# Three layers of an audio tower on one core: 258-token tiles with stacked scores against 512-token tiles with row-tiled scores

## The reference

```python
# 1. token mixer: per channel, over the time of a sequence
zf, zi, zh = x @ Wf + bf, x @ Wi + bi, x @ Wh + bh
diff = softplus(-zf) - softplus(-zi)
log_f, log_i = -softplus(diff), -softplus(-diff)
log_val = concat([log(0.5), log_i + log_g(zh)])        # now 257 positions
a_star = concat([0, log_f])
h = exp(a_star + cumlogsumexp(log_val - a_star))
# 2. attention with 8 heads of 16 channels; each sequence looks at the keys and
#    values of the one half a batch away
q, k, v = project(layernorm(h))
h = h + softmax(q @ swapped(k).T / sqrt(128)) @ swapped(v)
# 3. shared expert and 16 routed ones of 96 features, top 2 of 16
#    with f(a, b) = clip(a) * sigmoid(alpha * clip(a)) * scale * (clip(b) + shift)
x3 = layernorm(h)
z = f(x3 @ shared_w1 + shared_b1) @ shared_w2 + shared_b2
cw = normalised weights of the top 2 of softmax(x3 @ gate_w + gate_b), else 0
y = sum_e cw[e] * (f(x3 @ expert_w1[e] + expert_b1[e]) @ expert_w2[e] + expert_b2[e])
h = h + y + z
```

## Time and profile before

| | |
|---|---|
| median of three runs | 391.59 us |
| profiled execution: span from the first to the last instruction (the profile gives it no other time) | 388.2 us |
| instructions | 6049 |
| busy: TensorE, weight loads, VectorE, ScalarE, GpSimd | 316.8, 258.7, 298.8, 243.1, 158.3 us |
| granted TensorE clock, mean | 0.918 of 2.4 GHz |
| moved by DMA | 17.30 MB |

### The profile page before, as it was taken

One profiled execution on the slowest core, in us unless ns is written; L12 is line 12 of the kernel. 1 busy time (PEld: TensorE's weight loads), 2 busy tenths in 40 slices (PEclk: granted clock), 3 DMA queues, 4 the chain that ended last, 5 costly groups with the idle time before them and its releaser, 6 DMA issues. The chain is left out here.

```text
span 388.2 us, 6049 instructions
## 1 busy us (share of the span) xinstructions
PE 316.8 (82%) x2160; PEld 258.7 (67%) x2160; DVE 298.8 (77%) x500; ACT 243.1 (63%) x412; POOL 158.3 (41%) x125
## 2 busy tenths in 40 slices
PE   3427028986968999999899999979999998879873
PEld 1105027854667878788588787968787887768752
DVE  7894646722579969978998999887976788887990
ACT  2684521542684858597598685675773877485751
POOL 1000372101032874744348577342234445357752
PEclk9767755798986999999999999989999999999998
DMA  7500850000390000008400000075000000000000
GB/s 270 221 0 0 220 80 2 0 3 0 117 183 0 2 3 1 0 3 218 56 28 2 2 3 0 2 207 67 28 2 0 3 2 0 0 31 3 0 1 27
DMA packets 12414, 17.30 MB, mean 45 GB/s; under 512 B 984, under 2 KB 9184, under 8 KB 12256
## 3 DMA queue, kind: packets, MB, share of 16 engines
q1 hardware_dynamic: 12384, 16.91, 17.6%
HBM read 11.63 MB, written 5.28 MB: 44 GB/s over the span
## 5 line engine op out<-in xcount | busy, mean ns | idle before, releaser
L506 POOL TENSOR_TENSOR te<-tbuf,ubuf 128x516 f32<-128x516 f32 x52 | 73.8, 1424 | 50.4 <-DVE tbuf L882 27.6
L956 PE MATMUL slot<-xh,w1h 128*128 128x258 f32 x208 | 64.7, 311 | 13.0 <-DVE xl L865 4.0
L495 POOL TENSOR_TENSOR ubuf<-ubuf,cwb 128x516 f32<-128x516 f32 x24 | 34.3, 1429 | 67.2 <-ACT cwb L659 48.9
L956 PE MATMUL slot<-xh,w1l 128*128 128x258 f32 x208 | 59.9, 288 | 0.0
L956 PE MATMUL slot<-xl,w1h 128*128 128x258 f32 x208 | 59.8, 288 | 0.0
L956 PE MATMUL slot<-te,w 128*128 128x258 f32 x208 | 50.7, 393 | 4.2 <-POOL te L506 3.5
L956 PEld LDWEIGHTS slot<-xh,w1h 128*128 128x128 f32 x208 | 40.3, 194 | 19.4 <-issue 14.0
L882 DVE SCALAR_TENSOR_TENSOR tbuf<-tbuf,gbuf 128x516 f32<-128x516 f32 x52 | 48.3, 935 | 6.0 <-ACT tbuf L666 5.6
L781 DVE TENSOR_REDUCE mx<-slot 128x2 f32<-128x514 f32 x64 | 41.6, 687 | 12.6 <-PE slot L956 12.4
L956 PEld LDWEIGHTS slot<-te,w 128*128 128x128 f32 x208 | 39.6, 195 | 12.8 <-POOL te L506 6.4
L646 ACT ACTIVATE gbuf<-slot,cst 128x516 f32<-128x516 f32 x52 | 35.8, 690 | 19.2 <-PE slot L956 16.8
(11 more groups left out here) (161 smaller groups left out, 614.6 us busy)
## 6 DMA issues: line engine op xcount, KB each, us to landing
qs<-spill SPq DMA_DIRECT2D x12, 258.0 KB, 4.5
ks<-spill SPq DMA_DIRECT2D x24, 129.0 KB, 5.9
spill<-qhl SPq DMA_DIRECT2D x4, 516.0 KB, 2.8
spill<-khl SPq DMA_DIRECT2D x4, 516.0 KB, 3.4
pt<-in_w SPq DMA_DIRECT2D x1, 1664.0 KB, 9.5
xt<-in_x SPq DMA_DIRECT2D x4, 256.0 KB, 5.4
out<-osb SPq DMA_DIRECT2D x8, 128.0 KB
te<-in_sel SPq DMA_DIRECT2D x1, 832.0 KB, 11.0
```

The source lines that it names most:

```text
L495: g.tensor_tensor(ubuf[:, c % NB, :, :], ubuf[:, c % NB, :, :], cwb[:, :, :], ALU.mult).then_inc(S["ucw"], 1)
L506: g.tensor_tensor(te[:, c % NTE, :, :], tbuf[:, c % NB, :, :], ubuf[:, c % NB, :, :], ALU.mult)\
L956: return nc.tensor.matmul(out_, lhsT, rhs, start=start, stop=stop, **k)
```

## The change

The kernel is written anew around the same mathematics.

- **Tiles.** A unit has 2 x 256 = 512 tokens and no position 0. Since h is 0.5 there in every channel, its layer norm is 0, and so are its q, k and v: as a key it gives the score 0 (the products `e0` add its term to the denominator), as a query the plain mean of v. Its FFN is computed at the end for all eight sequences at once, in tiles of 8 columns (all pieces whose name begins with z, except `z` itself).
- **Mixer.** In logarithms: absolute value, exponential, logarithm on ScalarE, one product for half the difference of zi and zf (`lsum`, with `wd`), two scans, no reciprocal; all sums on VectorE for unit 0 and on GpSimd for the others, by `PART_BY` (`dw` always on VectorE).
- **Scores.** Nothing goes to memory and back. q and k are copied twice with every other head of 16 channels set to 0; a product takes 32 rows of them at partition 32t in f32, four of these (t = 0 to 3) one behind the other into four banks. The maximum goes into two rows of q through a transpose (`mz`, `nmt`, `nm`). The denominator's reciprocal is a logarithm and an exponential on ScalarE (`den`).
- **Experts.** 12 chunks hold 8 features of each of the 16 experts, so that partition p always belongs to expert p mod 16 and one tile `cwb` of routing weights serves all 12; a 13th chunk is the shared expert, with the weights in rows 96 to 111 for expert_b2. There are no selection products. The first bias is row 0 of the weights: `w1b` holds row 0 on all partitions, which is subtracted (`w1p`), and row 0 of the normalised input is set to 1. One half is now three products of 512 columns into one bank. The eviction clips at once (VectorE: all g, four of seven pairs of u; for the other pairs ScalarE copies and GpSimd clips). tanh, `gg`, the weighting `vc` (GpSimd) and `te` (now VectorE) run over pairs of chunks, 1024 elements.
- **PSUM and order.** Eight banks, each given by a table (`BANK_OF`), and a new `AT`.

The core of the difference:

```diff
-W = N + 1
+W = 2 * T
...
+GATE_BY = ("V", "V", "V", "V", "V", "V", "V")
+UP_BY = ("AG", "AG", "V", "AG", "V", "V", "V")
+CW_BY = ("G", "G", "G", "G", "G", "G", "")
+TE_BY = ("V", "V", "V", "V", "V", "V", "V")
+PART_BY = {"t": "VGGG", "d": "VGGG", "hg": "VGGG", "dw": "VVVV", "lf": "VGGG", "h1": "VGGG", "xl": "VVVV", "h2": "GGGG"}
+NY, NV, NT = 3, 3, 4
...
 AT = {
     "P": (
-        0, 2, 4, 3, 5, 6, 7, 8, 9, 13, 17, 11, 14, 15, 12, 16, 19, 23, 31, 32, 30, 25, 29, 26, 34, 35, 36, 37, 38, 39,
...
+        2, 1, 0, 3, 8, 11, 20, 15, 19, 21, 22, 26, 28, 29, 32, 30, 34, 23, 27, 31, 33, 39, 40, 35, 42, 45, 48, 52,
...
-            def stack_q(st, u):
-                if u == 0:
-                    sp.wait_ge(s_zero, 1)
-                ge(sp, "h2n", 2 * u)
-                sp.wait_ge(S["spill_q"], 16 * (u + 1))
-                for r, src in enumerate((0, 1, 0)):
-                    sp.dma_start(qs[32 * r:32 * r + 32, :, :, :].bitcast(F32),
-                                 spill[u][src].rearrange("(t p) s n -> p s t n", p=32)).then_inc(S["stack"], 16)
...
# TensorE
-            def max_(st, u, s, c, t):
-                name = ("max", s, c, t)
-                if (s, c, t) == (0, 0, 0):
-                    ge(pe, "stack", 16 * NSTACK * (u + 1))
-                    if u == 0:
-                        pe.wait_ge(s_zero, ZEROED)
-                        pe.wait_ge(s_hot, 1)
-                take(pe, st, name)
-                for i in range(2):
-                    last = mm(slot(st, name)[:, i, 0:W], qs[0:KR, s, t, c * P:(c + 1) * P], ks[0:KR, 1 - s, t, i, :])
-                fill(last, st, name)
...
+            def mx(u, s, c):
+                ps.released(pe, "q", u)
+                ps.released(pe, "k", u)
+                for t in range(PAIRS):
+                    ps.take(pe, "mx", u, s, c, t)
+                for i in range(2):
+                    for t in range(PAIRS):
+                        rows = slice(32 * t, 32 * t + 32)
+                        last = mm(ps.bank("mx", u, s, c, t)[:, i * T:(i + 1) * T], qt[rows, i, s, c * P:(c + 1) * P], kt[rows, i, 1 - s, :])
+                        if i:
+                            ps.fill(last, "mx", u, s, c, t)
...
-            def half_(st, u, c, k):
-                name = ("gu"[k], c)
-                ge(pe, "xl", u + 1)
-                if u == 0:
-                    pe.wait_ge(s_setd, SETUP)
-                take(pe, st, name)
-                for s in range(2):
-                    o = slot(st, name)[:, s, 0:W]
-                    mm(o, w1h[:, k, c, :], xh[:, s, :], stop=False)
-                    mm(o, w1h[:, k, c, :], xl[:, s, :], start=False, stop=False)
-                    last = mm(o, w1l[:, k, c, :], xh[:, s, :], start=False)
-                fill(last, st, name)
...
+            def half_(u, c, name, kind):
+                ge(pe, "xl", u + 1)
+                pe.wait_ge(s_w1l, W1_PARTS)
+                ps.take(pe, name, u, c)
+                o = ps.bank(name, u, c)[:, :]
+                cols = slice((2 * c + kind) * P, (2 * c + kind + 1) * P)
+                mm(o, w1h[:, cols], xh[:, u % 2, :], stop=False)
+                mm(o, w1h[:, cols], xl[:, u % 2, :], start=False, stop=False)
+                ps.fill(mm(o, w1l[:, cols], xh[:, u % 2, :], start=False), name, u, c)
...
-            def gate_half(st, u, c):
-                filled(act, st, ("g", c))
-                if c >= NB:
-                    ge(act, "gg", NF * u + c + 1 - NB)
-                release(a(gbuf[:, c % NB, :, :], slot(st, ("g", c))[:, :, 0:W], ACT.Identity, bias=par[:, B1G, c:c + 1]),
-                        st, ("g", c))
...
+            def up_copy(u, c):
+                n = NP * u + c // 2
+                ps.filled(act, "u", u, c)
+                te_done(act, n - NV)
+                last = a(vr[:, n % NV, c % 2, :], ps.bank("u", u, c)[:, :], ACT.Copy)
+                ps.release(last, "u", u, c)
...
+            def den(u, s):
+                tables(SET_EXP_LN)
+                ge(act, "pv", 4 * u + 2 * s + 2)
+                ge(act, "h2", 2 * (u - 1) + s + 1)
+                a(rden[:, s, :], ps.bank("o0", u, s)[:, T:W], ACT.Ln).then_inc(S["lden"], 1)
+                ge(act, "lden", 2 * u + s + 1)
+                a(rden[:, s, :], rden[:, s, :], ACT.Exp, scale=-1.0).then_inc(S["rd"], 1)
...
-            def clip_gate(st, u, c):
-                released(dve, st, ("g", c))
-                p = c % NB
-                v.tensor_scalar(gbuf[:, p, :, :], gbuf[:, p, :, :], fpar[:, GHI, c:c + 1], fpar[:, GLO, c:c + 1],
-                                ALU.min, ALU.max).then_inc(S["gclip"], 1)
...
+            def gate_evict(u, c):
+                n = NP * u + c // 2
+                ps.filled(dve, "g", u, c)
+                dve.wait_ge(s_par, PARS)
+                ge(dve, "gg", n - NY + 1)
+                r = col(c)
+                last = v.tensor_scalar(yr[:, n % NY, c % 2, :], ps.bank("g", u, c)[:, :], fpar[:, GHI, r:r + 1],
+                                       fpar[:, GLO, r:r + 1], ALU.min, ALU.max)
+                ps.release(last, "g", u, c)
...
+            def gg(u, k):
+                n = NP * u + k
+                ge(dve, "th", n + 1)
+                t = halves(k, tr, n % NT)
+                v.scalar_tensor_tensor(t, t, 1.0, halves(k, yr, n % NY), ALU.add, ALU.mult).then_inc(S["gg"], 1)
...
+            def w1p(u, k):
+                pool.wait_ge(s_w1s, 1)
+                pool.wait_ge(s_w1b, 16)
+                g.tensor_tensor(w1_raw[:, w1_part(k)], w1_raw[:, w1_part(k)], w1_row[:, w1_part(k)], ALU.subtract).then_inc(s_w1p, 1)
...
+            def up_clip(u, k):
+                n = NP * u + k
+                ps.released(pool, "u", u, chunks(k)[-1])
+                v_ = halves(k, vr, n % NV)
+                r = col(2 * k)
+                g.tensor_scalar(v_, v_, fpar[:, UHI, r:r + 1], fpar[:, ULO, r:r + 1], ALU.min, ALU.max).then_inc(S["ucg"], 1)
...
+            def weigh(u, k):
+                n = NP * u + k
+                clipped(pool, "u", UP_BY, n, "ucv", "ucg")
+                ps.released(pool, "cwb", u)
+                g.tensor_tensor(vr[:, n % NV, :, :], vr[:, n % NV, :, :],
+                                cwb[:, u % 2, :].unsqueeze(1).to_broadcast([P, 2, W]), ALU.mult).then_inc(S["vcg"], 1)
...
```

1755 lines of the change are left out of this document (973 added, 782 removed), and 112 rows, old and new, of tables (AT, BANK_OF, BY, ENGINES).

## The result

The changed kernel takes 325.18 us (median of four runs, 324.81 to 325.96) against 392.06 for the kernel before on the same chip (391.55 to 395.01): 0.8283 of its time, 95% interval 0.8251 to 0.8315. The forecast was 324 us. The profiled execution took 325.96 us with a span of 324.1, so 1.9 us lie around the span; the prediction's 3.4 compared a span with the median of other runs.

A forecast was written before the change was run, and what follows sets the result against it. It took ScalarE's list to set the opening, 90 us, and VectorE with 197 us at a share of 0.853 the rest, 231 us; with 3.4 us around the span that made 324 us, range 284 to 364.

The forecast's parts named there:

- The opening: Stretch ahead of the first 512-column half product: forecast to end at 90 us, against 108.66 before.
- with 7 us of waits: Opening: 8.4 us before ScalarE begins, 75 of its work and 7 of waits put the halves at 90 us.
- is hidden: Opening: loading and splitting the first-layer weights is covered by ScalarE's list; without that cover up to 12 us.
- TensorE's sum: Behind 90 us: halves, down, scores, position 0, tile shape changes and other products add up to 208 us.
- nothing here shows that four wide loads overlap: Scores: reason for taking 0.9 us per group of four, between bounds of 0.43 and 1.72; 34 us in all.
- VectorE's sum: Behind 90 us: VectorE's operations add up to 175 us, or 197 with `gg` and `te` stretched; 197 taken.
- The stretch of `gg` and `te`: VectorE behind 90 us: these operations slow as 935 to 695 while GpSimd works, 79 us instead of 59.
- 197/0.853 = 231 us: Behind 90 us: VectorE's 197 us at its earlier steady share of 0.853 gives 231 us.
- Rival 1: Everything packs: 0.43 us per score group, `gg` and `te` unstretched, halves from 80 us; 282 us, chance 0.20.
- Rival 2: Score row groups run one by one, 1.72 us per group, halves from 97 us; 357 us, chance 0.15.
- rival 4: Slower: row-tiled products do not pipeline, 0.76 us a product, halves at 123 us; 437 us, chance 0.05.
- Rival 3: Searched order does not fit real durations, VectorE's share falls to 0.72; 367 us, chance 0.12.

The follow-up runs named there:

- e3: Changed kernel with every score product (mx and st) issued twice into the same bank; 351.13 us against 325.18.
- e7: Changed kernel with GpSimd's eight `w1p` subtractions touching 8 instead of 416 columns each; 322.90 us against 325.18.
- e9: Changed kernel with all mixer sums of units 1 to 3 on VectorE instead of GpSimd; 337.02 us against 325.18.
- e8: Changed kernel with q and the first score pieces of unit 0 moved earlier in the order, in other banks; 323.00 us against 325.18.
- e10: e8's order carried on: all mx, both `nmt`, the first st and their softmax of unit 0 ahead of unit 3's token products; 332.33 us.
- e1: Changed kernel with VectorE's `te` multiplying only the first of the two chunks of a pair; 326.07 us against 325.18.
- e2: Changed kernel with each half made of two products instead of three (`w1l` product left out); 313.69 us against 325.18.
- e12: Changed kernel with e8's order and position 0's gate and up operands exchanged (8 columns stationary), in banks already free; 318.94 us against 325.18.
- e4: Changed kernel with score products issued two in a row on the same 32 rows instead of cycling over row groups; 325.98 us against 325.18.
- e6: Changed kernel with position 0's 78 narrow products spread, four behind each 512-column half product, instead of one block; 334.28 us against 325.18.

## Why the prediction was right, and where it was not

It was right in direction, in size and in where the gain would come from (behind the first half product). Its two parts were off by 20 and 17 us in opposite directions, so that 324 is partly luck.

**The opening, 90 us forecast, 109.7 measured.** ScalarE's list was sized well: 75 forecast, 69.8 busy. What failed is the step "with 7 us of waits". ScalarE is 0.64 busy ahead of the first half product, not above 0.8, and is idle for 40 us in all, 31 of them beyond the 8.4 ahead of its first work that the prediction allowed. It is a chain that crosses every engine: e3 (more TensorE work), e7 (less GpSimd work), e9 (more VectorE work), e8 and e10 (the order alone) all moved its end, by -3 to +11 us. A sum of the fullest engine's list is only a lower bound where four engines feed each other through eight banks. In 40 to 75 us TensorE's granted clock is 0.67, too, and 16 score records take 2.09 us in place of 1.15.

**The weights preparation "is hidden": half right.** No engine that computes waits for a transfer after 6.8 us. But leaving most of `w1p` out brought 3.1 us (e7), and `w1l` on VectorE took 12.9 us, not 8 x 0.6, in the engine that is fullest in the opening.

**TensorE's sum, 208 forecast, about 209 measured,** from row to row of its timeline. Inside it: scores 20.9 instead of 34 (a group 0.53, not 0.9); halves, with what changes of shape and low clock add to them, about 81 instead of 68 (0.233 apart, which was the upper bound, and a first one of 0.34 behind a change); position 0 18.5 instead of 12.5, since the clock falls in it; down 47 instead of 45; value and ones 21.9 instead of 20.9; the products of 512 f32 columns 8.4 and the small shapes 11.7, instead of 10.3 and 12.5. The bounds for a score group, 0.43 and 1.72, held, and the lower one was the nearer. The Trainium skill's page TensorE: Matmul & The Clock Gate (Part 3, Packing small matmuls) with its 3.07 gave an estimate of 0.56 a group; that was the better guide than "nothing here shows that four wide loads overlap". They do: 16 loads of 128 columns in 1.07 us are 0.067 each, below the 0.118 of the earlier trace rows.

**VectorE's sum, 197 forecast, 179.1 measured.** The prediction's own terms give 195 with the stretch, not 197 (175 - 59 + 79), which is 2 us of the 324. The stretch of `gg` and `te` (79 us assumed, 61.3 measured) did not come: 36 of the 48 ran while GpSimd stood still, and of the other 12 four were stretched, to 1.27 to 3.25 us. 175, the unstretched sum, was nearly right, by two errors that cancel: the two-sided clip from PSUM costs 0.80, not 0.69, 80 times, 8.8 us more, and the other rows together came out some 5 us less.

**"197/0.853 = 231 us": the step that failed.** It took VectorE as the engine that ends the time. Measured is 214.4: TensorE's 209, 1.6 of waiting (the expectations, which say 2.5, had counted one wait twice) and the last output's 4, while VectorE stands at 0.835. e1 shows that less VectorE work brings nothing, e2 and e3 that TensorE's does. The prediction's share of 0.90 for TensorE was too low; it is 208.7/214.4 = 0.97, where the same measure gives 253.9/279.5 = 0.91 before (the prediction's 220/279.5 = 0.79 is by dense distances and leaves out the 34 us by which the records are longer). e2 and e12 show how near the other bound is: with 24 us taken off TensorE, or its block of narrow products shortened, TensorE waits more for VectorE, 5.5 and 3.4 us where it was 1.6.

**The rivals.** Rival 1's conditions came true in two of three parts (row groups nearly side by side, `gg` and `te` unstretched), its 282 did not, because TensorE was then the bound and the opening was not 80 us. Rival 2 (1.72 a group) and rival 4 (no pipelining) are refuted by the spacing of the scores. Rival 3 as well: the searched order fits so well that TensorE waits 1.6 of 214 us.

## What to carry to other kernels

Where engines feed each other in a chain, add up the chain, not the fullest engine's list; where one engine waits for almost nothing, as TensorE here for 1.6 of 214 us, its sum of start-to-start distances is the time. Split the span at one event and compare variants by both parts: that shows at once which part a change touched. Narrow products did better in one block than spread (325 against 334 us), and better still with their operands exchanged once their banks were free (e12 against e8, 319 against 323 us); the banks of anything inserted must be ones already emptied, or the gain becomes a wait. When work leaves an engine, look at what then runs there earlier: in e9 the work that remained on GpSimd moved onto unit 0's mixer.

## What the runs showed of the hardware

- Two consecutive f32 products on the same 32 rows cost 1.09 against 1.07 us for a piece of eight that cycles over the row groups (e4); a repeated group of four costs 0.43 (e3).
- TensorE's clock can be low without a pause: with four 8-column records behind each 512-column product it was 1.2 GHz for 31 us, in which TensorE was never idle for more than 0.6 us (e6). It came back only in the run of 512-column products alone that followed. The fall itself came 1.3 us behind a wait of 2.7 us; in the kernel after it came inside the block of narrow products, without a wait.
- A VectorE operation with two SBUF inputs took 1.64 us in the mean in place of 0.58 while GpSimd did its sums (kernel after and e9), and two scans took 2.84 us in place of 1.32 (kernel after and e7); moving 17 us of sums from GpSimd to VectorE cost VectorE 4.8 us of busy time, though it made the opening longer.
- The two-sided clip with pointers, from PSUM, 512 columns: 798 to 812 ns in all 80 cases.
